# A ternary feed-forward layer joined to the retention program of a transformer kernel, with part of the next layer's preparation moved into the attention layer before it

## The reference, cut to what matters

```python
x = x + attention1(ln(x), ctx)          # 16 heads, softmax, projected by w_o
# layer 1, feed-forward: 8 adapters of rank 16, the best two of a softmax
x = x + adapters(ln(x))                 # route, relu(x @ Wd + bd) * weight, @ Wu + bu
# layer 2, attention: retention over the 8 tiles
k, v = heads(ctx, Wh), heads(ctx, Wh);  q = heads(ln(x), Wh)
x = x + (group_norm(mask(sum q k) v) * relu(ln(x) @ Wg)) @ Wo
# layer 2, feed-forward: ternary
def bitlinear(x, w):
    scale = 127 / max(max(abs(x), axis=-1), EPS)
    x_quant = clip(round(x * scale), -128, 127) / scale
    w_quant = clip(round(w * rms), -1, 1) / rms
    return x_quant @ w_quant.T
x = x + bitlinear(gelu(bitlinear(ln(x), w1)), w2)      # 256 -> 1024 -> 256
# layer 3: attention, then experts
```

## Time and profile before

| what | value |
|---|---|
| median of 3 runs | 1647.5 us (1647.1 to 1650.63) |
| the profiled execution's own time | 1647.25 us |
| its span, first to last instruction | 1645.4 us |
| PE busy over the span | 1494.5 us, 91% |
| DVE busy | 918.8 us, 56% |
| ACT busy | 739.8 us, 45% |
| POOL busy | 525.1 us, 32% |
| PE's mean granted clock | 0.966 of 2.4 GHz |

### The profile page before, as it was taken

The page is one execution under the profiler, slowest core; times in us unless marked ns, Lnnn a source line. Parts: engine busy times, 40 slices in busy tenths (PEclk is TensorE's granted clock), DMA queues, the critical chain, the costliest instruction groups (busy, mean ns, idle before and its releaser), DMA issues. The chain is left out here.

```text
span 1645.4 us, 22293 instructions
## 1 busy us (share of the span) xinstructions
PE 1494.5 (91%) x6989; PEld 1052.1 (64%) x6992; DVE 918.8 (56%) x2011; ACT 739.8 (45%) x2049; POOL 525.1 (32%) x507
## 2 busy tenths in 40 slices
PE   3989998999979999998999999998755999999998
PEld 1668776777754655556787878675623666654555
DVE  7787988888854342323455454545675555552221
ACT  3878787788852211111254434333333555552110
POOL 2566577877750000000452524121101333320000
PEclk9999999999998999999999999997967999999999
DMA  4201000200009000001000000002040000000000
GB/s 185 91 23 59 4 4 1 78 1 2 1 8 368 1 0 1 0 0 58 1 1 1 1 1 26 1 1 101 20 204 3 1 1 1 1 1 1 1 13 13
DMA packets 9716, 52.67 MB, mean 32 GB/s; under 512 B 1669, under 2 KB 3845, under 8 KB 6528
## 3 DMA queue, kind: packets, MB, share of 16 engines
q1 hardware_dynamic: 9008, 50.42, 7.9%
q0 software_dynamic: 160, 0.68, 0.2%
q10 hardware_dynamic: 432, 0.15, 0.0%
HBM read 50.87 MB, written 1.05 MB: 32 GB/s over the span
## 5 line engine op out<-in xcount | busy, mean ns | idle before, releaser
L1085 ACT ACTIVATE l0f_silu<-bank 128x512 f32<-128x512 f32 x48 | 28.7, 597 | 203.9 <-PE bank L1025 203.9
L1200 DVE TENSOR_TENSOR l0f_hidden<-l0f_product,bank 128x512 f32<-128x512 f32 x48 | 33.0, 688 | 155.3 <-PE bank L1036 155.3
L765 POOL TENSOR_TENSOR l0a_stepped<-l0a_y,l0a_m 128x512 f32<-128x512 bf16 x64 | 76.2, 1190 | 106.8 <-DVE l0a_m L567 106.5
L787 POOL TENSOR_TENSOR l0a_head_rstd<-l0a_head_var,all_minus_half 128x4 f32<-128x4 f32 x96 | 102.3, 1069 | 12.8 <-DVE l0a_head_var L586 12.7
L2077 PE MATMUL bank<-l3a_f_xn_t,all_weights_b 128*128 128x512 f32 (+1 forms) x208 | 94.0, 594 | 1.7 <-DVE all_weights_a L2260 1.7
L718 ACT ACTIVATE l0a_work<-bank,l0a_neg_max 128x128 f32<-128x128 f32 x256 | 90.2, 369 | 6.3 <-DVE l0a_neg_max L599 6.1
L1025 PE MATMUL bank<-l0f_xn_t,all_weights_b 128*128 128x512 f32 x192 | 92.2, 603 | 0.0
L1025 PE MATMUL bank<-l0f_xn_t,all_weights_a 128*128 128x512 f32 x192 | 90.8, 596 | 0.0
L1562 DVE TENSOR_TENSOR all_weights_a<-bank,all_cols 128x512 f32<-128x512 f32 x64 | 44.0, 690 | 83.7 <-PE bank L1419 83.5
L1047 PE MATMUL bank<-all_weights_a,l0f_hidden 128*128 128x256 f32 x384 | 90.5, 378 | 0.0
L438 PE MATMUL bank<-all_ident,l0a_work 128*128 128x128 f32 x384 | 61.3, 283 | 31.9 <-DVE l0a_work L594 30.9
(11 more groups left out here) (405 smaller groups left out, 3845.2 us busy)
## 6 DMA issues: line engine op xcount, KB each, us to landing
all_weights_a<-in_l_w_q SPq DMA_DIRECT2D x2, 2048.0 KB, 15.0
all_weights_b<-in_l_e_gate SPq DMA_DIRECT2D x1, 3072.0 KB, 10.6
all_weights_a<-in_l_e_up SPq DMA_DIRECT2D x4, 768.0 KB, 10.3
all_weights_a<-in_l_e_down SPq DMA_DIRECT2D x1, 3072.0 KB, 18.2
all_weights_b<-in_l_w_qx SPq DMA_DIRECT2D x1, 2048.0 KB, 11.5
all_weights_b<-in_l_w_proj_x SPq DMA_DIRECT2D x1, 2048.0 KB, 17.9
all_weights_b<-in_l_w_proj SPq DMA_DIRECT2D x1, 2048.0 KB, 9.2
all_weights_b<-in_l_w_q SPq DMA_DIRECT2D x1, 2048.0 KB, 8.3
```

What stands on the lines that cost most here:

```text
L765: done = g.tensor_tensor(stepped[:, 0:n], value, step, ALU.add)
L787: g.tensor_tensor(head_rstd[:, m % 2, :], head_var[:, m % 2, :], res.minus_half[:, 0:HU], ALU.pow)\
```

## The change

The function `layer2_ternary` goes; its work stands in the block of adapters and retention, now `layer1_adapters_to_layer2`. The input rows of the ternary layer are normalised and rounded by pairs of tiles, those of pairs 0 and 1 between the gates and sums of the retention's tail. Rounding to 1024 values is split: DVE makes the maximum and scale (`scale_of_act`), ACT multiplies and adds the rounding constant (`scale_act`), DVE subtracts it, clips at 127 and writes bf16 (`finish_act`). The lower clip at -128 is gone in both roundings. There are four gelu buffers in place of two, and two output banks in place of one. SP issues layer 3's loads in four parts, each behind a semaphore. The normalised rows of tiles 0 to 5 for the adapters, and the four retention-key products, are made in the last period of layer 1's attention, and `l2_heads` is loaded with that layer's other weights. The diff, cut to its core:

```diff
@@ layer1_attention @@
+    LAST_OUT = SCORE[-1] + 7
+    L2_KEYS = [LAST_OUT - 1 + n for n in range(4)]
+    F_TILES = TILES - 2
+            def project_l2_keys(p, n):
+                if p < PAIRS:
+                    return
+                h, half = divmod(n, 2)
+                if n == 0:
+                    pe.wait_ge(res.loaded["l2_heads"], 16)
+                wait_ring_free(pe, p, "k2", n)
+                pe.matmul(ring_bank(p, "k2", n)[:], res.place["l2_heads"][:, h, :], ctx_t[:, 2 * half:2 * half + 2, h, :],
+                          start=True, stop=True).then_inc(ring_made.sem, 1)
-                                   (project_out, later(SCORE, 7))])
+                                   (project_out, later(SCORE, 7)), (project_l2_keys, L2_KEYS)])
+            def f_variance(period, _):
+                if period == PAIRS:
+                    v.drain()
+                    v.tensor_scalar(res.f_var[:, 0:F_TILES], res.moments[:, 0:F_TILES, 1], 1e-5, None, ALU.add)\
+                     .then_inc(f_var_ready, 1)
+            def f_row(period, t):
+                if period == PAIRS:
+                    if t == 0:
+                        v.wait_ge(f_rstd_ready, 1)
+                        scored.wait(v, scored.at(PAIRS - 2, NA))
+                    v.tensor_scalar(res.f_rows[:, t, :], res.x[:, t, :], res.moments[:, t, 0:1], res.f_rstd[:, t:t + 1],
+                                    ALU.subtract, ALU.mult)
             march(PERIODS, STEPS, [(row_max, SCORE), (row_inverse, later(SCORE, 2)), (key_variance, later(KEY_SUM, 0)),
+                                   (f_variance, [STEPS - 8]), (f_row, [STEPS - 6 + t for t in range(F_TILES)]),
...
+            def keep_l2_keys(p, n):
+                if p == PAIRS:
+                    h, half = divmod(n, 2)
+                    ring_made.wait(act, last_count("k2", n))
+                    act.activation(res.l2_keys[:, h, half * HALF:(half + 1) * HALF], ring_bank(p, "k2", n)[:], ACT.Copy)\
+                       .then_inc(l2_keys_kept.sem, 1)
             march(PERIODS, STEPS, [(keep_mixed, later(SCORE, 6)), (exponentials, SCORE), (keep_probs, later(SCORE, 4)),
+                                   (keep_l2_keys, L2_KEYS),
...
@@ layer1_adapters_to_layer2, SP @@
             loads(sp)
+            sp.wait_ge(values_kept, 4)
+            late_loads[0](sp)
+            sp.wait_ge(weights_rounded, 1)
+            late_loads[1](sp)
+            sp.wait_ge(x_done, PAIRS)
+            late_loads[2](sp)
+            sp.wait_ge(t_x_done, TILES)
+            late_loads[3](sp)
...
@@ PE, after the mixes @@
+            project_out(2)
+            turn_in(0)
+            project_out(3)
+            wide(0)
+            wide(1)
+            turn_in(1)
+            for t in range(2, TILES + 4):
+                if t < TILES:
+                    wide(t)
+                if t % 2 == 1 and t // 2 + 1 < PAIRS:
+                    turn_in(t // 2 + 1)
+                if 3 <= t < TILES + 3:
+                    turn_act(t - 3)
+                if t >= 4:
+                    narrow(t - 4)
...
@@ ACT @@
+            def scale_act(t):
+                act.wait_ge(act_inv_ready, t + 1)
+                act.activation(act_rows[t % 4], act_rows[t % 4], ACT.Identity, bias=magic[:],
+                               scale=act_inv[:, t:t + 1]).then_inc(act_scaled, 1)
+            keep_in(0)
+            gelu(0)
+            keep_in(1)
+            gelu(1)
+            for t in range(TILES + 1):
+                if t < TILES:
+                    scale_act(t)
+                if 2 <= t + 2 < TILES:
+                    gelu(t + 2)
+                if t >= 1:
+                    keep_act(t - 1)
+                if t % 2 == 1 and (t + 3) // 2 < PAIRS:
+                    keep_in((t + 3) // 2)
...
@@ DVE @@
+            def round_in(p):
+                pair, tiles = slice(2 * p, 2 * p + 2), (2 * p, 2 * p + 1)
+                v.wait_ge(in_rstd_ready, p + 1)
+                row_pair(in_rows, in_rstd, p)
+                v.tensor_reduce(in_max[:, pair], in_rows[:, pair, :], X, ALU.max, apply_absolute_value=True)
+                v.tensor_scalar(in_step[:, pair], in_max[:, pair], T_EPS, 1.0 / 127.0, ALU.max, ALU.mult)
+                v.reciprocal(in_inv[:, pair], in_step[:, pair])
+                v.tensor_scalar(in_scale[:, pair], in_step[:, pair], ternary.rms[:, 0:1], None, ALU.mult)
+                for t in tiles:
+                    v.tensor_scalar(in_round[:, t % 2, :], in_rows[:, t, :], in_inv[:, t:t + 1], ROUND_INT, ALU.mult, ALU.add)
+                v.tensor_scalar(in_q[:, p % 2, :, :], in_round[:], ROUND_INT, 127.0, ALU.subtract, ALU.min).then_inc(in_q_ready, 1)
...
+            def scale_of_act(t):
+                v.wait_ge(gelu_done, t + 1)
+                a = act_rows[t % 4]
+                v.tensor_reduce(act_max[:, t:t + 1], a, X, ALU.max, apply_absolute_value=True)
+                v.drain()
+                v.tensor_scalar(act_step[:, t:t + 1], act_max[:, t:t + 1], T_EPS, 1.0 / 127.0, ALU.max, ALU.mult)
+                v.drain()
+                v.reciprocal(act_inv[:, t:t + 1], act_step[:, t:t + 1]).then_inc(act_inv_ready, 1)
+                v.tensor_scalar(act_scale[:, t:t + 1], act_step[:, t:t + 1], ternary.rms[:, 1:2], None, ALU.mult)
+            def finish_act(t):
+                a = act_rows[t % 4]
+                v.wait_ge(act_scaled, t + 1)
+                if t >= 2:
+                    v.wait_ge(act_turned, t - 1)
+                v.tensor_scalar(act_q[:, t % 2, :], a, ROUND_INT, 127.0, ALU.subtract, ALU.min).then_inc(act_q_ready, 1)
             open_gate(0)
+            open_gate(1)
+            add_to_x(0)
+            open_gate(2)
+            add_to_x(1)
+            round_in(0)
+            open_gate(3)
+            add_to_x(2)
+            round_in(1)
+            add_to_x(3)
+            for t in range(TILES + 3):
+                if t < TILES:
+                    scale_of_act(t)
+                if 1 <= t <= TILES:
+                    finish_act(t - 1)
+                if t % 2 == 0 and t // 2 + 2 < PAIRS:
+                    round_in(t // 2 + 2)
+                if t >= 3:
+                    add_narrow(t - 3)
...
-    "l2_heads": ("a", 0, (2, P)), "l2_gate": ("a", 256, (KC, D)), "l2_out": ("a", 768, (KC, D)),
+    "l2_heads": ("b", 4624, (2, P)), "l2_gate": ("a", 256, (KC, D)), "l2_out": ("a", 768, (KC, D)),
...
+                                          [loader(res, w, *names) for names in (("l3_e_gate", "l3_e_up"), ("l3_w_o",),
+                                                                                ("l3_w_q", "l3_route"), ("l3_e_down",))])
```

More of the change, by code:

```diff
@@ L2436, in round, with layer1_adapters_to_layer2 @@
         eng.drain()
-def adapters_and_retention(nc, top, res, w, ternary, loads):
+def layer1_adapters_to_layer2(nc, top, res, w, ternary, loads, late_loads):
     E, ANNEALED = 8, 3.0 * (1.0 - 1 / 625)
     GN_EPS = 0.001
+    T_EPS, F = 1e-5, 1024
+    FC = F // P
     HALVES, HALF, PAIRS, WIDE = 2, 4 * P, TILES // 2, 2 * P
     with phase_memory(nc, "mid") as mem:
-        f_xn_t, f_rows = view(res.wb, 0, KC, TILES * P), view(res.wb, 2048, TILES, D)
-        relu, hidden, weight_t = (view(res.wb, 5120 + i * 1024, HALVES, HALF) for i in range(3))
+        f_xn_t, f_rows, k_t = view(res.wb, 0, KC, TILES * P), res.f_rows, res.l2_keys
+        relu, hidden, weight_t = (view(res.wb, start, HALVES, HALF) for start in (5120, 2048, 3072))
         squares = res.wa[:, 8192:10240]
@@ L2734, in _ @@
             turn(0)
[L2735 to L2738 removed]
+            turn(1)
+            project_out(0)
+            turn(2)
+            project_out(1)
+            turn(3)
+            project_out(2)
[13 more added lines that the diff above has]
+                    narrow(t - 4)
         @block.scalar
@@ L3110 @@
+            for p in range(PAIRS):
+                pair = slice(2 * p, 2 * p + 2)
+                g.wait_ge(in_var_ready, p + 1)
+                g.tensor_tensor(in_rstd[:, pair], in_var[:, pair], res.minus_half[:, pair], ALU.pow).then_inc(in_rstd_ready, 1)
 PLACES = {
```

407 lines of the change are left out of this document (172 added, 235 removed).

## The result

The changed kernel took **1618.4 us** in the median of four runs (1617.3 to 1623.9) against 1647.5: a ratio of 0.9826 [0.9814, 0.9839]. Run again later, beside other kernels, it took 1616.3 us (1615.4 to 1616.6), ratio 0.9805 [0.9791, 0.9820]. The profiled execution took 1618.3 us with a span of 1616.5, 28.9 less than the 1645.4 of before.

What follows compares the result with a forecast made beforehand. The prediction took DVE to bound the ternary layer, with PE bounding the attention before it and the retention's middle. Front 2.9 + joined stage 19.75 - last issue 0.4 = 22.2 us gained, giving 1625.5 us, range 1620 to 1634.

Steps and rivals of the forecast that it cites:

- the two stretches up to ScalarE's last kept turn: Joined ternary stage: VectorE bounds up to scale(3) at 1210.2, then ScalarE to 1227.3; 14.8 and 17.1 us.
- The weights' turn: Adapters, after the gate: without the keys ahead of it, it starts about 1134.9 instead of 1136.77, a gain of 1.9 us.
- the front's clock: Adapters' entry: full clock in turns and routing gains 0 to 4.5 us, half clock later loses up to 4; taken as 0.
- The joined stage: Retention's tail and ternary layer: the last sum ends at 1230.5 instead of 1250.25, a gain of 19.75 us before 0.4 off.
- the closing: End of the ternary layer: last down product, 1.9 us at 1.2 GHz or about 1.0 at full clock, and the sum.
- The two delays in attention: Attention's end: a moved row ahead of the last reciprocal costs 0.35 us, the first key product sticks out by about 0.2.
- the first turn: Adapters' entry: PE begins at about 1116.1 instead of 1116.90; with 0.2 for no pair-by-pair feeding, a gain of 1.0 us.
- The gap at the block's end: After the last ternary sum: SP's last load issue stands behind that sum and delays the block's end by 0.4 us.
- slower: Ternary layer: table switches above about 1.9 us each outweigh DVE's gain; 1653 us at 2.5 us each; chance 0.02.
- PE becomes the bound: Ternary layer: at half clock PE needs 4.5 us per tile against ACT's 3.8, 6.5 us later, 1632 us; chance 0.13.
- Tables switched: Ternary layer: gelu and Identity in different tables add about 12 loads of 1.28 us on ACT, 1639 us; chance 0.05.
- The front gives nothing: Attention's tail and adapters: moved work delays the tail, PE falls to half clock; 2.9 us lost and more, 1629 us; chance 0.06.

Runs made afterwards that it cites:

- Experiment 1: Kernel before, nothing moved, plus five idle TensorE products around the pause ahead of the adapters' first turn: 1642.8 us against 1648.1, ratio 0.9968.
- experiment 2: Changed kernel with both moves to attention's end undone (rows and key products back in the adapters' block): 1627.4 us, ratio 0.9877 to the kernel before.
- experiment 3: Kernel before with only the two moves to attention's end (rows of tiles 0 to 5, four key products): 1643.1 us, ratio 0.9972.
- experiment 4: Changed kernel with only the key products put back into the adapters' block, rows still moved: 1623.4 us, ratio 0.9850 to the kernel before.
- experiment 5: Changed kernel with only the adapters' rows put back into their own block, keys still moved: 1627.3 us, ratio 0.9873 to the kernel before.
- experiment 8: Changed kernel with two idle TensorE products of 512 columns in the retention's tail: 1617.1 us, ratio 0.9814; unchanged copy 1616.3 us.
- experiment 9: Changed kernel with four idle TensorE products around the start of layer 3: 1614.4 us, ratio 0.9803; unchanged copy 1616.3 us.
- experiment 10: Changed kernel with the load of layer 3's last expert weights issued by layer 3's own SyncE program: 1617.9 us, ratio 0.9818.
- experiment 11: Changed kernel with that late load moved to layer 3 and idle products in retention's tail, ahead of the fourth ternary tile and around layer 3's start: 1616.6 us, ratio 0.9810.
- experiment 6: Changed kernel with the scaling of the 1024 values back on VectorE instead of ScalarE: 1628.2 us, ratio 0.9867 to the kernel before.

## Why the prediction was wrong

**What was right.** VectorE bounded the ternary layer, and ScalarE's scaling, the joint and the clip that is gone took its work or waits away. ScalarE bounds from the fourth tile on, and no table is switched. `round_in` takes 3.2 (predicted 3.3), the scaling 1.25 (1.2), the two stretches up to ScalarE's last kept turn 14.5 and 17.15 (14.8 and 17.1). The weights' turn, freed from the keys, gained 2.0 (1.9). The first maximum came 26.5 us behind the first statistics of the retention (1186.05 - 1159.53), predicted 26.4; that was in part luck, as the same code did it in 24.3 when the clock held.

**The step that failed is the front's clock: "I take 0 for the two together".** The bounds were 4.5 us gained and 4 lost, as if they cancelled. The gain was 4.7 us, all of it on the path, because the clock held from attention's end through the turns and the logits. The loss hardly came. In the first profile the clock was at 0.57 in 1120 to 1124, under the down projections, where the gate and not TensorE sets the time. In the repeat it fell later, the spread products took 3.2 us instead of 2.0, and A's last part was 33.2 instead of 32.2: a loss of 1.0, and in no trace 4. Had the term been +4.5 and -0.5, the sum would have been 26.2 us and the forecast 1621.5. Experiment 1 shows the clock's gain without any moved work, 3.4 us in its trace, and 2 to 5 show that it needs both moves.

**The whole difference.** The profiled gain was 28.9 us, the sum 22.2. Of the 6.7 between them A holds 5.5 (8.4 against 2.9), B 1.3 (20.7 against 19.35) and the stretch ahead of A 1.1; C took 1.3 away.

**The joined stage was undersized.** 82.2 - 19.35 makes 62.85 for B; it took 61.5 and 58.5, and 58.0 to 60.5 in experiments 2, 4, 5 and 8 to 11, whose order of this stage is the changed one. By the parts of B, the closing is the term that was always too large: one down product and one sum made 1.6 us instead of 3.2, with the product at 1.05 us, full clock, where the forecast mixed 1.9 and 1.0. In the repeat ScalarE's phase was 0.75 shorter as well: the forecast added durations, but starts lie closer. In the first profile a wait of 0.84 us for a wide product took that back. And the retention's tail was 24.3 to 24.6 us in seven traces, with a clock of 1.00 in its first 8 us, and 26.2 to 26.6 with 0.83 to 0.92 in experiments 5 and 6 and the first profile. That is worth 2.2 us, which no term of the sum held.

**Small terms.** The two delays in attention, 0.35 and 0.2, didn't come. The last projection follows its mixes by 1.75 us in both kernels (1107.36 to 1109.11, 1106.26 to 1108.01), since the key product fits the 0.69 us that TensorE waited there. And the changed kernel is 1.1 us ahead of the one before at 805 us and at the last projection alike, so the rows cost nothing. With these 0.55 us back, the first turn came 1.6 us earlier in A instead of 1.0. The gap at the block's end grew by 0.77 (1.60 against 0.83), predicted 0.4; experiment 10 shows 0.5 of it to be the issue. Layer 3, at which I had looked for no change, took 0.7 to 1.3 more: the granted clock of its first 16 us was 0.57, before 0.68. And in the rival called slower, 24 / 12 is 2.0 us per switch and not 1.9; nothing hangs on it.

**The rivals.** *PE becomes the bound*: out; the granted clock was 0.60 in 1190 to 1200, 0.88 in the next 10 us and 1.00 after, while first VectorE and then ScalarE set the pace. *Tables switched* and with it *slower*: out; sixteen gelus and eight Identities with one load of 1283 ns, and twelve loads in the whole kernel before and after. The Trainium skill, *ScalarE: Activation LUTs*, section on table sets, says that identity is filler in every set, and by that the trace agrees. *The front gives nothing*: out, 8 us of A. The range failed at its low end: the front's -4.5 was in it, yet the closing, the delays that didn't come and the clock ahead of A came on top of it.

## What to carry to other kernels

A stage that crawls at half clock behind a pause of TensorE is worth as much as the instructions removed: ask what would fill or shorten that pause, and try it with idle products before any code is moved. Two moves that each shorten a pause a little can bring next to nothing of this alone and all of it together, so cost them as a pair. Sum a chain on one engine from start to start, not from durations. And before a difference between two stages is put down to an edit, split the stage where the edit begins: in experiment 6 a quarter of it lay ahead of that.

## What the runs showed of the hardware

TensorE kept 2.4 GHz through turns and eight-column products after a pause of 1.6 us, and was at 1.2 GHz in the eight-column products after pauses of 3.7, 4.0 and 5.8 us; after that of 4.0 the first turn still ran at 2.4 (1.07 us for eight). It isn't a rule without exceptions: in experiment 6, with the same pause of 1.6, turns and logits took 7.0 us, as the clock fell before the last sixteen logits were made (3.15 us; 1.91 in the changed kernel).

```profile
1122.40 3.15 PE L2647 MATMUL bank<-all_weights_b 128*128 128x8 f32 x16
```

Unchanged code lost or gained up to 2.3 us in the retention's tail and up to 4.7 ahead of the change, by where the dips of the granted clock fell. A gain in one stage can stand beside a loss in stages that nobody touched (experiment 3: 8.4 gained, 6.8 lost in the profiled execution), so an experiment here is read by stages, and its whole time only beside several runs.
